# Identity products in the gaps of TensorE at both ends, key sums applied to the masked matrix, and a re-chosen order, in a four-layer sequence kernel

## The reference

```python
# layers 0 and 3 (heads: 16 and 8)
xn = layernorm(x)
q, k, v = xn @ Wq + bq, xn @ Wk + bk, xn @ Wv + bv       # k masked to -inf or -1e6, v masked to 0
q = softmax(q, axis=features_of_a_head)
k = softmax(k, axis=tokens)
att = einsum('bnhd,bnhl->bhdl', k, v)                    # one small matrix per head
y = einsum('bnhd,bhdl->bnhl', q, att)
x = x + silu(layernorm(y) * (1 + scale) + shift) @ W_out + b_out
# layers 1 and 2 (512 channels, 16 states)
u = silu(conv4(xn @ W_in));  dt = softplus(...);  B, C from u @ W_x
h = h * exp(dt * A) + dt * u * B;  y = sum_over_states(h * C)     # a scan over the 512 tokens
x = x + gate * ((y + u * D) * silu(z)) @ W_out
```

## Time and profile before

| what | us |
|---|---|
| median of three runs | 2191.97 |
| the profiled execution | 2192.97 |
| its span | 2191.2 |
| DVE busy | 1941.5 |
| POOL busy | 1825.9 |
| PE busy | 1888.3 |
| ACT busy | 1728.4 |

### The profile page before, as it was taken

One profiled execution on the slowest core, in us unless ns is written; L12 is line 12 of the kernel. 1 busy time (PEld: TensorE's weight loads), 2 busy tenths in 40 slices (PEclk: granted clock), 3 DMA queues, 4 the chain that ended last, 5 costly groups with the idle time before them and its releaser, 6 DMA issues. The chain is left out here.

```text
span 2191.2 us, 22191 instructions
## 1 busy us (share of the span) xinstructions
PE 1888.3 (86%) x5712; PEld 957.1 (44%) x5712; DVE 1941.5 (89%) x2014; ACT 1728.4 (79%) x3140; POOL 1825.9 (83%) x906
## 2 busy tenths in 40 slices
PE   7967779899988989899998989899998988688786
PEld 5533335445453534545353444445454443334354
DVE  5479999999999999999998999999998999989952
ACT  2387778998988889898888988898888987667642
POOL 0088998989898998989898898989899798989940
PEclk8888999999999999999999999999999999889997
DMA  6065564656565665655566475655556566556620
GB/s 243 1 181 167 172 197 144 188 169 178 155 176 165 167 202 157 199 153 169 154 181 175 146 211 163 180 163 164 170 160 177 165 194 168 175 158 190 191 59 20
DMA packets 170541, 358.73 MB, mean 164 GB/s; under 512 B 19544, under 2 KB 27952, under 8 KB 161712
## 3 DMA queue, kind: packets, MB, share of 16 engines
q1 hardware_dynamic: 151958, 279.32, 39.2%
q0 software_dynamic: 9216, 67.11, 15.4%
q10 hardware_dynamic: 9242, 10.89, 1.5%
HBM read 284.85 MB, written 5.29 MB: 132 GB/s over the span
## 5 line engine op out<-in xcount | busy, mean ns | idle before, releaser
L755 POOL TENSOR_TENSOR state<-state,c_rows 128x1024 f32<-128x1024 f32 x512 | 1224.1, 2437 | 144.4 <-DVE state L1310 98.5
L1613 PE MATMUL bank<-state,const_sb 128*128 128x512 f32 x1536 | 767.4, 617 | 86.3 <-POOL state L755 78.6
L1310 DVE TENSOR_TENSOR_SCAN state<-decay,mix_banks 128x512 f32<-128x512 f32 x640 | 754.1, 1208 | 27.8 <-ACT decay L1033 11.1
L1307 DVE TENSOR_TENSOR_SCAN state<-mix_banks,state 128x512 f32<-128x512 f32 x384 | 449.3, 1204 | 44.5 <-POOL state L746 22.0
L746 POOL TENSOR_TENSOR state<-kept,b_rows 128x1024 f32<-128x1024 f32 x192 | 466.8, 2438 | 8.4 <-DMA b_rows<-flat_rows 5.7
L1613 PEld LDWEIGHTS bank<-state,const_sb 128*128 128x128 f32 x1536 | 281.0, 195 | 406.3 <-issue 226.4
L1033 ACT ACTIVATE decay<-kept,ssm_pack 128x512 f32<-128x512 f32 x640 | 433.9, 710 | 2.3 <-ACT x_dbl L972 1.2
L1300 DVE TENSOR_TENSOR mix_banks<-kept,mix_banks 128x1024 f32<-128x1024 f32 x320 | 393.0, 1228 | 17.6 <-ACT mix_banks L1025 7.4
L1017 ACT ACTIVATE mix_banks<-kept,ssm_pack 128x512 f32<-128x512 f32 x384 | 256.0, 681 | 108.5 <-DVE state L1310 88.7
L1511 PE MATMUL bank<-kept,ssm_pack 128*128 128x512 f32 x512 | 249.5, 621 | 26.1 <-DVE kept L1259 9.2
L1025 ACT ACTIVATE mix_banks<-b_rows 128x512 f32<-128x512 f32 x320 | 188.5, 592 | 58.7 <-DVE state L1310 30.0
(11 more groups left out here) (195 smaller groups left out, 2197.6 us busy)
## 6 DMA issues: line engine op xcount, KB each, us to landing
b_rows<-flat_rows SPq DMA_DIRECT2D x512, 256.0 KB, 3.9
c_rows<-flat_rows SPq DMA_DIRECT2D x512, 256.0 KB, 3.7
state<-state POOLq DMA_DIRECT2D x64, 1024.0 KB, 10.1
out<-x_res ACTq DMA_DIRECT2D x8, 512.0 KB, 6.0
ssm_pack<-ssm_pack SPq DMA_DIRECT2D x2, 2035.0 KB, 12.1
x_next<-x ACTq DMA_DIRECT2D x6, 512.0 KB, 6.6
state<-ada_w SPq DMA_DIRECT2D x1, 1536.0 KB, 11.7
kept<-ada_w SPq DMA_DIRECT2D x1, 1536.0 KB, 14.1
```

The source lines that it names most:

```text
L755: pool.tensor_tensor(st, st, by_pair(c_rows[:, row % ROWS]), ALU.mult).then_inc(m_prod, 1)
L1307: ins = dve.tensor_tensor_scan(st, mixed, st, 0.0, ALU.mult, ALU.add)
L1310: ins = dve.tensor_tensor_scan(st, decay[:, nth(g) % DECAYS], mixed, 0.0, ALU.mult, ALU.add)
L1613: pe.matmul(y_banks[c2][:], ident, state[:, g % STATES], start=False, stop=(g == in_bank[-1])).then_inc(m_sum, 1)
```

## The change

Three things are done.

1. Identity products that nobody reads, the fillers, are put on PE by `fill`: 128 by 128 by 128 in fp32, into a bank of the preparations. There are 18, 20 and 14 in attention 0 (ahead of `turn0`, `k0` and `yT0`), 10 ahead of the first preparation's turn, and 26, 6, 30 and 10 in attention 15 (ahead of `turn0`, `k0`, `yT0` and `out0`). Ahead of the 26 PE also waits until DVE has read the last bank of the last evaluation.
2. In the eight attentions of layer 3 the two multiplications of `kexp` by `krec` on ACT are gone; PE's turns of `kexp` wait for the exponentials alone. DVE's one multiplication of `att` by the head mask becomes two `scalar_tensor_tensor`, each 128 by 128, which multiply by `krec` and by the mask.
3. Nearly all numbers of the tables that set the order are new, and so are the stretches of the setup, of the first preparation, of the first woven attention, of the last two attentions and of the last evaluation.

```diff
-SETUP_UNITS, FIRST_PREP, FIRST_ATT = (-107, -45), (-82, 16), (-73, 31)
+SETUP_UNITS, FIRST_PREP, FIRST_ATT = (-104, -42), (-74, 15), (-74, 31)
-LATE_ATTS, FIRST_TAIL_END, LAST_POST_END = ((156, 218), (265, 304)), 26, 24
+LATE_ATTS, FIRST_TAIL_END, LAST_POST_END = ((156, 217), (238, 294)), 26, 29
...
-    "bank": (1, 3, 4, 4, 4, 4, 3, 4, 4, 4, 5, 2, 4, 4, 4, 4, 1, 3, 4, 4, 0, 2, 4, 4, 4, 4, 2, 3, 4, 4, 4, 4),
+    "bank": (0, 2, 4, 4, 4, 4, 3, 4, 4, 4, 4, 1, 4, 4, 4, 4, 2, 3, 4, 4, 4, 2, 4, 4, 4, 4, 1, 3, 4, 4, 4, 4),
...
+FILLERS = {(0, "turn0"): 18, (0, "k0"): 20, (0, "yT0"): 14, (ATTENTIONS - 1, "turn0"): 26, (ATTENTIONS - 1, "k0"): 6,
+           (ATTENTIONS - 1, "yT0"): 30, (ATTENTIONS - 1, "out0"): 10}
+PREP_FILLERS = 10
...
+ROWS_SCALED = [attention_index(3, b) for b in range(B)]
+
+
+def columns_scaled_before(ai):
+    return ai - sum(k < ai for k in ROWS_SCALED)
...
                 yield from w.to("q0")
-                for c in range(DC):
+                if layer == 0:
                     act.wait_ge(a_krec, ai + 1)
-                    act.activation(kexp[:, c, :], kexp[:, c, :], ACT.Copy, scale=krec[:, c:c + 1]).then_inc(a_kn, 1)
+                    for c in range(DC):
+                        act.activation(kexp[:, c, :], kexp[:, c, :], ACT.Copy, scale=krec[:, c:c + 1]).then_inc(a_kn, 1)
...
-                dve.tensor_tensor(att[:], pa[:, 0:DC * P].rearrange("p (c n) -> p c n", c=DC),
-                                  aw(layer, "heads").unsqueeze(1).broadcast_to([P, DC, P]), ALU.mult).then_inc(done, 1)
+                if layer == 0:
+                    dve.tensor_tensor(att[:], pa[:, 0:DC * P].rearrange("p (c n) -> p c n", c=DC),
+                                      aw(layer, "heads").unsqueeze(1).broadcast_to([P, DC, P]), ALU.mult).then_inc(done, 1)
+                else:
+                    dve.wait_ge(a_krec, ai + 1)
+                    for c in range(DC):
+                        ins = dve.scalar_tensor_tensor(att[:, c, :], pa[:, c * P:(c + 1) * P], krec[:, c:c + 1],
+                                                       aw(layer, "heads"), ALU.mult, ALU.mult)
+                    ins.then_inc(done, 1)
...
+            def fill(count):
+
+                for _ in range(count):
+                    pe.matmul(pb[1][:, 0:P], ident, ident, start=True, stop=True)
+
...
                 for c in range(DC):
                     yield from w.to(f"turn{c}")
+                    if (ai, f"turn{c}") in FILLERS:
+                        if ai == ATTENTIONS - 1:
+                            taken(pe, post_fill(SCANS - 1, "gather1"))
+                        fill(FILLERS[ai, f"turn{c}"])
                     pe.wait_ge(a_xn, 2 * ai + 1)
...
-                    pe.wait_ge(a_kn, ai * DC + DC)
+                    if layer == 0:
+                        pe.wait_ge(a_kn, columns_scaled_before(ai) * DC + DC)
+                    else:
+                        att_taken(pe, ai, "k0", "k1")
...
+                if pi == 0:
+                    fill(PREP_FILLERS)
                 pe.wait_ge(p_xn, pi + 1)
```

More of the change, by code:

```diff
@@ L83 @@
 ATT_STAGES = by_name(ATT_NAMES, {
-    "first": (108, 9, 5, 15, 5, 45, 67, 55, 7, 20, 23, 12, 0, 17, 54, 41, 0, 36, 42, 68, 8, 43, 29, 47, 14, 61, 7, 10,
-              13, 61, 76, 4, 86, 52, 12, 38, 15, 161, 107, 12, 61, 29, 62, 14, 37, 78, 104, 20, 31, 70, 27, 102),
-    "second": (11, 15, 0, 49, 4, 33, 39, 51, 0, 9, 35, 18, 24, 19, 25, 48, 41, 3, 8, 94, 18, 54, 102, 40, 78, 21, 16,
[9 rows of a table removed]
-    "late": (4, 2, 51, 7, 3, 19, 14, 29, 0, 6, 11, 0, 6, 19, 9, 0, 17, 7, 8, 7, 13, 19, 8, 17, 0, 9, 11, 0, 22, 0, 8,
-             26, 2, 11, 0, 10, 7, 18, 47, 10, 11, 16, 20, 19, 10, 10, 38, 21, 37, 25, 46, 0),
@@ L98 @@
-    "last": (6, 17, 18, 75, 84, 24, 100, 55, 9, 4, 99, 13, 9, 5, 94, 115, 2, 15, 77, 1, 19, 0, 59, 3, 36, 56, 49, 24,
-             25, 67, 6, 12, 32, 16, 12, 65, 50, 92, 120, 20, 0, 7, 26, 12, 33, 32, 42, 43, 6, 5, 82, 65),
+    "first": (68, 61, 1, 20, 24, 21, 70, 42, 56, 53, 20, 6, 8, 55, 50, 17, 5, 70, 43, 85, 14, 42, 21, 38, 5, 76, 2, 3,
+              2, 33, 36, 59, 115, 17, 0, 41, 23, 185, 108, 14, 39, 43, 76, 16, 15, 71, 114, 0, 12, 69, 47, 90),
+    "second": (32, 13, 1, 44, 8, 27, 28, 38, 33, 10, 53, 1, 49, 30, 7, 48, 44, 11, 6, 76, 15, 45, 121, 45, 64, 48, 1,
[9 rows of a table added]
@@ L100 @@
+    "late": (19, 7, 51, 14, 0, 18, 9, 7, 24, 5, 8, 7, 9, 32, 10, 9, 24, 2, 12, 9, 5, 21, 4, 4, 15, 10, 13, 4, 11, 2,
+             4, 34, 0, 12, 13, 23, 0, 18, 43, 16, 12, 11, 27, 26, 6, 2, 33, 50, 30, 37, 60, 2),
+    "last": (5, 7, 40, 61, 76, 6, 116, 80, 17, 25, 103, 5, 18, 3, 94, 111, 21, 3, 80, 0, 4, 4, 87, 35, 32, 21, 39, 3,
+             29, 100, 16, 72, 18, 24, 13, 51, 51, 73, 95, 56, 18, 6, 51, 5, 16, 14, 65, 42, 22, 26, 63, 69),
 })
 PREP_STAGES = by_name(PREP_NAMES, {
-    "first": (76, 5, 39, 28, 14, 53, 20, 12, 16, 5, 2, 36, 62, 9, 18, 7, 17, 31, 36, 71, 6, 23, 28, 22),
[4 rows of a table removed]
+    "first": (73, 24, 25, 32, 0, 67, 0, 2, 2, 40, 15, 1, 58, 29, 32, 0, 47, 15, 30, 49, 12, 35, 34, 19),
[4 rows of a table added]
@@ L107 @@
 })
 POST_STAGES = by_name(POST_NAMES, {
[4 rows of a table removed]
-    "last": (7, 10, 7, 27, 37, 15, 28, 23, 26),
[4 rows of a table added]
+    "last": (2, 12, 4, 41, 9, 31, 64, 8, 34),
 })
 TAIL_STAGES = by_name(TAIL_NAMES, {
-    "first": (105, 50, 7),
-    0: (83, 5, 3),
-    1: (33, 25, 23),
-    2: (20, 4, 19),
-    3: (19, 11, 0),
+    "first": (102, 66, 18),
+    0: (98, 18, 26),
+    1: (69, 12, 0),
+    2: (51, 0, 23),
+    3: (40, 22, 26),
 })
-SETUP_STAGES = dict(zip(SETUP_NAMES, (17, 7, 0, 9, 5, 17, 55, 21, 17, 35, 6, 69, 32), strict=True))
+SETUP_STAGES = dict(zip(SETUP_NAMES, (24, 19, 3, 8, 12, 27, 57, 13, 1, 23, 24, 66, 28), strict=True))
@@ L131 @@
+    "row": (4, 4, 3, 4, 5, 4, 4, 4, 5, 4, 4, 4, 2, 4, 4, 4, 4, 4, 3, 4, 4, 4, 3, 4, 5, 4, 4, 4, 3, 4, 1, 4),
+    "beside": (5, 5, 7, 4, 4, 3, 5, 5, 8, 4, 5, 5, 9, 8, 8, 7, 5, 5, 7, 6, 5, 5, 11, 8, 0, 2, 5, 5, 8, 9, 1, 3),
+    "inject": (7, 5, 5, 5, 5, 5, 8, 5, 5, 5, 8, 5, 5, 5, 5, 5, 6, 5, 5, 5, 4, 5, 5, 5, 5, 5, 8, 5, 5, 5, 5, 5),
+    "weight": (4, 6, 5, 6, 7, 6, 6, 6, 2, 6, 4, 6, 6, 6, 8, 6, 5, 6, 2, 6, 3, 6, 3, 6, 5, 6, 5, 6, 6, 6, 6, 6),
 }
@@ L1425, in attention @@
                     if e == 0:
+                        fill(FILLERS.get((ai, "k0"), 0))
                         pe.wait_ge(s_key_bias, 1)
@@ L1466, in attention @@
                     yield from w.to(f"yT{c}")
+                    fill(FILLERS.get((ai, f"yT{c}"), 0))
                     pe.wait_ge(a_xn, 2 * ai + 2)
@@ L1470, in attention @@
                     yield from w.to(f"out{h}")
+                    fill(FILLERS.get((ai, f"out{h}"), 0))
                     att_taken(pe, ai, "yT0", "yT1")
```

4 lines of the change are left out of this document (removed), and 34 rows, old and new, of tables (ATT_STAGES, POST_STAGES, PREP_STAGES).

## The result

The changed kernel takes 2156.68 us (median of four runs, 2155.7 to 2162.63) against 2191.59 us for the kernel before in the same series (2190.29 to 2193.4): a ratio of 0.9848, 95% interval [0.9823, 0.9873]. The forecast was 2182 us with a range of 2170 to 2192, so the gain of 35 us is over three times what was forecast and lies outside the range. The direction was right. Rival (c), a gain in the body by fewer waits, named the right cause and gave it 15 us and a chance of 0.12.

A forecast was written before the change was run, and what follows sets the result against it. DVE was taken to bound the body, chains of short steps the two ends. Start -2.5, body -3, end -4.2 and keys' sums 0 gave -9.7 us: 2183.3 from the profiled execution, 2182 against the median, range 2170 to 2192.

The forecast's parts named there:

- Rival (c): Body: gains more, some 15 us, by fewer waits for ACT and PE, giving 2170 us; chance 0.12.
- The new order in the body: Body: no operation added or removed, only DVE's idle time moves; -3 us, bounds -12 and +25.
- The keys' sums: Eight attentions: ACT loses 11.3 us of work, DVE's pairs add 1.4 us, relief worth the same; sum 0.
- The start: Up to the first scan: fillers make slow PE products fast; -2.5 us, bounds -6 and +3.
- The end: Attention 15: fillers gain 1.5 us at keys, 2.9 at out products, longer `att` costs 0.2; -4.2 us, bounds -6.5 and 0.
- (a): Body: DVE waits out ACT's unit 0 decay, issued with no lead, in each half scan; 22 us longer, 2207; chance 0.13.
- (b): Body: gives the ends' gain back, +3 to +11 us there, about 2191 us in all; chance 0.15.
- (d): Start and end: fillers do not hold the clock and run at 0.48 us; about +20 us, 2212; chance 0.02.

The follow-up runs named there:

- b_both: The kernel before with the changed kernel's stage tables and half-step leads, without keys' sums and fillers; 2170.5 us, ratio 0.9901.
- four mixed sets: Stage tables or half-step leads exchanged singly between the kernel before and the changed kernel; 2236.94, 2218.04, 2210.64 and 2237.91 us.
- a_keys: The changed kernel with the inverse key sums applied as before, by ACT copies and one DVE product; 2169.33 us, ratio 0.9912.
- after: The changed kernel itself, with all parts of the change; 2156.68 us, ratio 0.9848 to the kernel before.
- b_keys: The kernel before with the inverse key sums applied on the masked matrix in eight attentions, nothing else; 2193.18 us, ratio 1.0012.
- a_bank0: The changed kernel with one lead put back: unit 0's decay issued one half step ahead again; 2155.29 us.

## Why the prediction was wrong, step by step

**The new order in the body: the step that failed.** The prediction took -3 us, with ends at -12 and +25. Measured, against the body of before: -22 for the tables alone (b_both), -33 with the keys' sums, and +13 to +48 for the four mixed sets. The direction was right, the size was not: the prediction called itself wrong if DVE's idle time in the body moved by over 8 us, and it moved by 26.8. I see three reasons; no run splits the 22 us among them. First, I took DVE's waits for small ones with no one cause, and saw 10 us of waits for PE. The four rows were only the top of the list: the waits for PE were 37.0 us in the body, and they are what the tables brought down (22.8 in b_both). And the tables repeat, so a place that they mend is mended in three or four half scans at once, as the table of half scans shows. Second, I priced a wait at its length on DVE. The chains above show that it starts as 4.26 us on ACT or 2.48 on PE, passes to whatever stands behind, and is doubled where PE has idled and its clock has fallen; PE's busy time in the body was 1732 us before and 1713 in the changed kernel (1722 in its second profile), for the same products. Third, the lower end of -12 rested on "some hundred waits of 1 us", when the view gave the real bound, 122 us of idle time of DVE, of which 27 went.

**The keys' sums: the second step that failed.** The prediction took 0, as ACT was not the bound and the relief would be worth the 1.4 us of DVE's pairs. The pair was sized right: two L1232 take 0.61 us, forecast 0.6. The relief was wrong: 9.4 us in the body by a_keys against after. I counted ACT's 11.3 us of work and looked for who waits for it. What counted was that the copies made ACT wait, in the middle of its list, for a reciprocal far down DVE's. In the kernel before that wait was 6.7 us in all, and b_keys shows the edit worth nothing there. The new tables would have made it 15.4. The edit gains only with the tables, and a price for each part alone could not have found this.

**The start: wrong in sign, small.** Forecast -2.5 within -6 and +3; measured +1.1. The fillers were 0.23 us each at the high clock (4.63 us for the 20), and the keys did run fast (1.97 us at 16.13 against 3.56). But the 14 stood behind 52 records of 8-column products (6.0 us), not behind 20, and ran partly slow, 4.72 us, between the 3.4 and 6.7 of the forecast; and the clock was down again where attention 1 begins. What the fillers were to bring there, some 4 us less behind them, did not reach the first scan.

**The end: right.** Forecast -4.2, measured -5.3. In the timeline of the changed kernel:

```profile
2104.65 6.07 PE L1399 MATMUL bank<-const_sb 128*128 128x128 f32 x52 [0.79 <-DVE x_res L1304]
2108.00 1.38 DVE L1170 TENSOR_SCALAR xn<-x_res,att_minus,att_rstd 128x256 f32<-128x256 f32 x4 [1.22 <-POOL att_rstd L708]
2110.56 0.60 PE L1416 MATMUL bank<-const_sb,xn 128*128 128x128 f32 x4
2112.98 1.95 PE L1422 MATMUL mix_banks<-xnT,att_pack 128*128 128x512 f32 x4
2131.66 0.61 DVE L1232 SCALAR_TENSOR_TENSOR att<-bank,krec,att_pack 128x128 f32<-128x128 f32 x2 [5.50 <-PE bank L1485]
2134.39 6.86 PE L1399 MATMUL bank<-const_sb 128*128 128x128 f32 x60
2141.09 0.60 PE L1416 MATMUL bank<-const_sb,xn 128*128 128x128 f32 x4
2144.83 1.13 PE L1435 MATMUL mix_banks<-att_pack,xnT 128*128 128x256 f32 x4
2148.64 1.13 PE L1435 MATMUL bank<-att_pack,xnT 128*128 128x256 f32 x4
```

The turn was ready at 2109.38 (2108.00 + 1.38) and started at 2110.56, 1.2 us late (forecast 1.4). From there to the end of the keys' bias, 2117.48, are 8.1 us from ready, where the earlier trace rows had 9.76: 1.7 gained, forecast 1.5. The 30 fillers took 6.86 us, not 7.2, and made the second turn 1.1 us late, not 1.7. From ready (2139.97) to the end of the last out product (2149.77) are 9.8 us, where it had been 13.4 (from 2173.61 to 2187.05): 3.6 gained, forecast 2.9. Together the two gains are the 5.3 us. The rise of the clock that the Trainium skill, "TensorE: Matmul & The Clock Gate", section "What's actually happening", calls variable from run to run does not show at this end: the end's length agrees within 0.2 us over eleven profiles. It may show at the start, where the first scan of the same stages and fillers moves over 5 us; no run separates it from other causes there.

**The rivals.** (a) fell (a_bank0). (b) and (d) did not occur; fillers ran at 0.11 to 0.12 us a record at the end. (c) was the case, at twice its size. Its chance was too low: it shared its cause with the forecast, and nothing in the profile set the border between them at 8 us.

## What to carry to other kernels

A table that orders in-order engines is priced by the idle time that it can reach, not by a count of waits: a fifth of the bound engine's idle time was won here, mixed tables lost 13 to 48 us of the body, and one table of the matched set alone told nothing of the whole. Where one engine works through a list, look for the instruction in it that waits longest for a late neighbour, and ask what stands behind it; taking that away was worth 9 us here, while the same work without the wait was worth little. Fillers pay ahead of a short chain of products that all wait for each other (4.8 us at the end), and not where the clock has time to fall again before the work that counts.
